# Attention and dense experts in one block: rows prepared tile by tile in attention's loop, first dense steps among its last slots

## The reference, cut to what matters

```
x = x + attention(layernorm(x), ctx)       # 16 heads, self and cross; LN; fp8 rounding of the
                                           # projections' inputs and of the head outputs
h = layernorm(x)                           # rows of x again: mean, variance, (x - m) * rstd
logits = h @ router_w                      # 8 experts, the best 2, softmax of the two
combined = sum over the row's 2 experts of score * (silu(h @ w1g[e]) * (h @ w1u[e])) @ w2[e]
shared = (silu(h @ w_gate) * (h @ w_up)) @ w_down      # "dense": every row, 1,024 wide
x = x + combined + shared
```

## Time and profile before

| | us |
|---|---|
| median of 3 runs (lowest, highest) | 1046.34 (1046.0, 1047.96) |
| the profiled execution, its own time | 1046.31 |
| its span in the trace | 1044.6 |
| PE busy | 960.6 (92%) |
| DVE busy | 796.8 (76%) |
| ACT busy | 737.8 (71%) |
| POOL busy | 434.2 (42%) |
| mean granted clock of TensorE | 0.972 |

### The profile page before, as it was taken

One profiled execution on the slowest core, in us unless ns is written; L12 is line 12 of the kernel. 1 busy time (PEld: TensorE's weight loads), 2 busy tenths in 40 slices (PEclk: granted clock), 3 DMA queues, 4 the chain that ended last, 5 costly groups with the idle time before them and its releaser, 6 DMA issues. The chain is left out here.

```text
span 1044.6 us, 23638 instructions
## 1 busy us (share of the span) xinstructions
PE 960.6 (92%) x7238; PEld 679.7 (65%) x7239; DVE 796.8 (76%) x1691; ACT 737.8 (71%) x1345; POOL 434.2 (42%) x642
## 2 busy tenths in 40 slices
PE   5487999999999999999999999859999799999994
PEld 3364777777777777777777777626565556666663
DVE  7677999999999999999999999766887634444441
ACT  6776888888888888888888878357455444454552
POOL 5223454445444544454445444270256013233222
PEclk9798999999999999999999999969999999999997
DMA  9924001010010010100100101041266364222222
GB/s 253 251 78 81 22 22 40 20 40 20 20 40 20 20 40 20 34 26 20 42 21 22 42 21 42 1 145 58 83 211 198 129 178 88 25 25 26 28 27 26
DMA packets 32821, 65.46 MB, mean 63 GB/s; under 512 B 3712, under 2 KB 20736, under 8 KB 32512
## 3 DMA queue, kind: packets, MB, share of 16 engines
q1 hardware_dynamic: 23312, 50.20, 15.4%
q0 software_dynamic: 9456, 14.59, 8.1%
HBM read 53.42 MB, written 16.59 MB: 67 GB/s over the span
## 5 line engine op out<-in xcount | busy, mean ns | idle before, releaser
L595 POOL TENSOR_TENSOR root<-vareps,neghalf 128x4 f32<-128x4 f32 (+1 forms) x128 | 173.7, 1357 | 10.0
L588 POOL TENSOR_TENSOR var<-ssq,unit 128x4 f32<-128x4 f32 (+1 forms) x128 | 52.6, 411 | 280.6 <-DVE ssq L455 280.6
L326 PE MATMUL b_pj<-w_hi,xq 128*128 128x512 f16 x384 | 148.7, 387 | 2.1 <-DVE xq L578 1.5
L399 ACT ACTIVATE sq<-b_pj 128x512 f32<-128x512 f32 x192 | 114.0, 594 | 50.6 <-PE b_pj L326 49.5
L326 PE MATMUL b_pj<-w_lo,xq 128*128 128x512 f16 x384 | 147.8, 385 | 0.0
L455 DVE TENSOR_REDUCE ssq<-sq 128x4 f32<-128x512 f32 x192 | 130.1, 678 | 11.2 <-ACT sq L399 11.1
L466 DVE TENSOR_TENSOR nrm<-raw,rstd 128x512 f32<-128x512 f32 x192 | 128.3, 668 | 5.1 <-POOL rstd L599 4.4
L1539 POOL DMA_INDIRECT out<-xg x39 | 60.5, 1552 | 169.2 <-ACT xg L1641 153.9
L352 PEld LDWEIGHTS b_sc<-kT,qT 128*128 128x128 f32 x1024 | 123.1, 192 | 7.2 <-ACT qT L425 0.3
L342 PE MATMUL b_tr<-ident,nrm 128*128 128x128 f32 x768 | 117.2, 276 | 9.7 <-DVE nrm L466 9.3
L352 PE MATMUL b_sc<-kT,qT 128*128 128x64 f32 x1024 | 121.5, 272 | 0.0
(11 more groups left out here) (291 smaller groups left out, 2288.0 us busy)
## 6 DMA issues: line engine op xcount, KB each, us to landing
nst<-in_ffw SPq DMA_DIRECT2D x30, 512.0 KB, 3.3
wload<-in_ffw SPq DMA_DIRECT2D x30, 512.0 KB
xbuf<-zero SPq DMA_DIRECT2D x39, 129.0 KB, 2.8
xg<-xbuf SPq DMA_DIRECT2D x9, 516.0 KB
x_sb<-in_x SPq DMA_DIRECT2D x4, 512.0 KB, 13.7
wproj<-in_ctxT SPq DMA_DIRECT2D x1, 2048.0 KB, 9.9
xq<-in_w_all SPq DMA_DIRECT2D x4, 512.0 KB, 21.3
wproj<-in_wprojT POOLq DMA_DIRECT2D x4, 512.0 KB, 8.9
```

What stands on the lines that cost most here:

```text
L326: last = pe.matmul(o, x, w[:, k, at:at + BANK], start=(k == 0 and n_ == 0), stop=(k == KT - 1 and n_ == len(terms) - 1))
L399: act.activation(sq[:, (r * NN + c) % 2, :], b_pj[c % 2][:, :], ACT.Square).then_inc(s["sq_done"], 1)
L595: pool.tensor_tensor(root[:, r % 2, c, :], vareps[:, r % 2, c, :], neghalf[:, 0:1].unsqueeze(2).to_broadcast(shape), ALU.pow).then_inc(s[" ...
```

## The change

- One block for attention and dense experts. The work on a tile's rows moves into attention's loop with offset `ROWS = -5`, one part per slot: in slots N%4 = 1 DVE's moments and then four POOL instructions (`pool_rows`); in N%4 = 2 the high half on ACT, the low half on DVE into `xr`; in N%4 = 3 four PE transposes into the bank of the probabilities and one ACT eviction into `xhl`. The router's four matmuls stand ahead of an output projection. `xr` goes to a DRAM buffer tile by tile; one 2,048 KB load brings all rows back as `xn`, behind weight piece 6 of SP's loads.
- The loop body is two tiles (8 slots), looped from slot 8 to 47, and the ring of quantised rows holds 2 tiles.
- The context is split in five parts: tile 0, then tiles 1 to 3, and 4, 4 and 4, one part in each of slots 0 to 3. Each quarter of `wproj`'s weights is loaded behind its part.
- Dense `up(0)` to `up(6)` go into slots 61 to 67, half behind "project 0", half behind "project 1"; `down(0)` into slot 65, 1 and 2 into 66, 3 and 4 into 67. They use attention's banks. Pieces 0 to 5 are split in slots 59 to 65, `silu` stands from slot 62 on, `product(n)` at the end of DVE's slot 62+n.
- In the dense steps left, the router's choice stands at step 7 (before 4), the end of the routing at 17 (before 14), weight pieces at steps 6, 7, 9, 10, 12 and up. A scatter waits for four dense steps more. `xg0` lies in the low half of `xhl` and waits for all dense ups and all scatters.

```diff
-        RING = 13
+        RING = 2
+        LOOPED = (2, 12)
...
+            def pe_rows(pe, t, part):
+                if part != 2:
+                    return
+                pe.wait_ge(s["xn_done"], t + 1)
+                after(pe, "xh_done", t)
+                after(pe, "ptev_done", min(4 * t + 8, 4 * NT) if isinstance(t, int) else 4 * t + 8)
+                for a in range(2):
+                    for k in range(KT):
+                        last = pe.transpose(b_t[:, a, k, :], xr[:, a * H + k * P:a * H + (k + 1) * P], ident16[:, :])
+                last.then_inc(s["t3_done"], 1)
...
-                    (0, "raw 2"): context_high,
+                    (0, "raw 2"): lambda: context_high(1), (1, "raw 2"): lambda: context_high(2),
+                    (2, "raw 2"): lambda: context_high(3), (3, "raw 2"): lambda: context_high(4),
...
+            def pool_rows(pool, t, part):
+                if part:
...
+                after(pool, "xn_done", t)
+                pool.wait_ge(s["mv3_done"], t + 1)
+                pool.tensor_tensor(ve3[:, :], mv3[:, 1:2], epsc[:, 0:1], ALU.add).then_inc(s["ve3"], 1)
+                pool.wait_ge(s["ve3"], t + 1)
+                pool.tensor_tensor(rs3[:, :], ve3[:, :], neghalf[:, 0:1], ALU.pow).then_inc(s["rs3"], 1)
+                pool.tensor_tensor(n3, row(x_sb, t), mv3[:, 0:1].to_broadcast([P, H]), ALU.subtract).then_inc(s["n3_sub"], 1)
+                pool.wait_ge(s["n3_sub"], t + 1)
+                pool.wait_ge(s["rs3"], t + 1)
+                pool.tensor_tensor(n3, n3, rs3[:, 0:1].to_broadcast([P, H]), ALU.mult).then_inc(s["n3_pool"], 1)
...
-            PIECE_SLOTS = (4, 6, 7) + tuple(range(11, NS))
+            PIECE_SLOTS = (6, 7, 9, 10) + tuple(range(12, NS))
...
                     sp.dma_start(stage[n % 3][:, :], ffw[n, :, :]).then_inc(s[f"wst_in{n % 3}"], 16)
+                    if n == 4:
+                        store_rows(sp, NT - 2)
+                    if n == 6:
+                        store_rows(sp, NT - 1)
+                        sp.wait_ge(s["row_out"], 16 * NT)
+                        sp.wait_ge(s["proj_done"], 16 * NT)
+                        sp.dma_start(xn[:, :, 0:2 * H].bitcast(U32), rowbuf).then_inc(s["rows_in"], 16)
                 sp.wait_ge(s["scattered"], 16 * 2 * NT)
-                sp.dma_start(xg0[:, :, :].bitcast(U32), x_rows[:, 0:TURN, :]).then_inc(s["xg_in"], 16)
+                sp.wait_ge(s["gu_done"], NS)
+                sp.dma_start(xg0.bitcast(U32), x_rows[:, 0:TURN, :])\
+                    .then_inc(s["xg_in"], 16)
...
-                        pool.wait_ge(s["gu_done"], (NT * slot + t) // 2 + 12)
+                        pool.wait_ge(s["gu_done"], (NT * slot + t) // 2 + 16)
...
+                def first_gate(n):
+                    def run():
+                        if n == 0:
+                            pe.wait_ge(s["xh_done"], 4)
+                            pe.wait_ge(s["raw_done"], 16 * NT)
+                        if n == 1:
+                            pe.wait_ge(s["tev_done"], NN * 4 * NT)
+                        pe.wait_ge(s["wl_done"], 2 if n < 4 else 4)
+                        after(pe, "a_done", n - 1)
+                        up_part(0, 0, n)
+                    return run
...
+                for n in range(JOIN + 1):
+                    tail[FIRST - 1 + n, "project 0"] = first_gate(n)
+                    tail[FIRST - 1 + n, "project 1"] = first_up(n)
+                tail[FIRST + 3, "project 3"] = downs(0)
+                tail[FIRST + 4, "first transposes"] = expert_sums
+                tail[FIRST + 4, "project 3"] = downs(1, 2)
+                tail[FIRST + 5, "project 3"] = downs(3, 4)
+                attention_tensor(pe, tail)
...
+                tail = {(FIRST - 3, "tokens"): shared(0), (FIRST - 2, "raw 1"): shared(1), (FIRST - 1, "raw 3"): units_known}
+                for n in range(JOIN):
+                    tail[FIRST + n, "first eviction"] = lambda n=n: gate(act, 0, n)
+                    tail[FIRST + n, "rows"] = lambda n=n: high(act, 0, n)
...
+                tail = {(FIRST - 2, "token norm"): shared(0), (FIRST - 2, "squares 2"): shared(1),
+                        (FIRST + 2, "tokens"): expert_scales}
+                for n in range(JOIN):
+                    if n:
+                        tail[FIRST + n, "token norm"] = lambda n=n: low(dve, 0, n - 1)
+                    tail[FIRST + n, "rows"] = lambda n=n: product(dve, 0, n)
+                for n in range(2, 6):
...
+                    (7, "weights"): choose, (8, "weights"): indices, (9, "weights"): marks,
+                    (10, "weights"): scores_and_counts, (11, "weights"): tile_scans,
+                    (12, "weights"): expert_scans, (13, "weights"): rows, (14, "weights"): tiles,
+                    (15, "weights"): codes, (16, "weights"): expert_units, (17, "weights"): expert_units_end,
                 })
```

More of the change, by code:

```diff
@@ L102, in rstd3 @@
[L102 to L108, removed]
+        st3 = sb("st3", [P, 6], F32)
+        mv3 = sb("mv3", [P, 2], F32)
+        ve3 = sb("ve3", [P, 1], F32)
+        rs3 = sb("rs3", [P, 1], F32)
@@ L271, in slots, with store_rows, attention_sync @@
                             between[N]()
-                        slot(N // 4, N % 4)
-                slots(-3, 4)
-                with eng.Fori(1, RING - 2) as i:
-                    for r in range(4):
-                        slot(i, r)
-                slots(4 * (RING - 2), 4 * NT + 3)
-            @block.sync
-            def _(sp):
+                        slot(N // 4, N % 4, N // 4 % 2)
+                first, end = LOOPED
+                slots(-3, 4 * first)
+                if 4 * first in between:
+                    between[4 * first]()
+                with eng.Fori(first, end, 2) as i:
+                    for r in range(8):
+                        slot(i + r // 4, r % 4, r // 4)
+                slots(4 * end, 4 * NT + 4)
+            def store_rows(sp, t):
+                sp.wait_ge(s["xn_done"], t + 1)
+                sp.dma_start(rowbuf[:, t, :], xr[:, :].bitcast(U32)).then_inc(s["row_out"], 16)
+            def attention_sync(sp):
                 sp.dma_start(col[:, :], cols).then_inc(s["cols_in"], 16)
@@ L1144, in ranks, with up_part @@
                     pe.matmul(b_rank, before, both.rearrange("p a b -> p (a b)"), start=True, stop=True)
-                    pe.matmul(b_tot, ones, both.rearrange("p a b -> p (a b)"), start=True, stop=True)\
+                    pe.matmul(b_tot, ones[:, :], both.rearrange("p a b -> p (a b)"), start=True, stop=True)\
                         .then_inc(s["rank_done"], 1)
+                def up_part(c, g, f):
+                    n = NF * g + f
+                    w, b = ((sw[0], b_g), (sw[1], b_u))[c]
+                    for k in range(KT):
+                        for m, (part, xx) in enumerate(((0, xh), (0, xl), (1, xh))):
+                            last = pe.matmul(b[f % 2][:, :], w[part][:, k * SF + f * P:k * SF + (f + 1) * P],
+                                             xx[:, k, g * BANK:(g + 1) * BANK],
+                                             start=(k == 0 and m == 0), stop=(k == KT - 1 and m == 2))
+                    if c:
+                        last.then_inc(s["gu_done"], 1)
                 def up(pe, g, f):
@@ L1174, in down, with downs @@
                     last.then_inc(s["ys_done"], 1)
-                def both_of(a, b):
+                def downs(*steps):
                     def run():
-                        if a is not None:
-                            route(a)
-                        if b is not None:
-                            turn(b)
-                    return run
-                pe.wait_ge(s["ones_set"], 1)
-                pe.wait_ge(s["wjob_done"], 1)
-                pe.matmul(b_wt, ones, wjob[:, :], start=True, stop=True).then_inc(s["wtot_done"], 1)
@@ L1750, in pieces, with halves @@
         return w.reshape(-1, PIECE // w.shape[1], P, w.shape[1]).transpose(0, 2, 1, 3).reshape(-1, P, PIECE)
+    def halves(w):
+        return w.reshape(KT, P, 2, SF // 2).transpose(2, 1, 0, 3).reshape(2, P, PIECE)
+    dense = [half for pair in zip(halves(w_gate), halves(w_up)) for half in pair]
     experts = [part for e in range(E) for part in (pieces(w1[e]), pieces(w2[e]))]
     arrays["router_w"] = np.ascontiguousarray(inputs["L0_ffn_router_w"])
-    arrays["ffw"] = np.ascontiguousarray(np.concatenate([pieces(w_gate), pieces(w_up), pieces(w_down)] + experts))
+    arrays["ffw"] = np.ascontiguousarray(np.concatenate([np.stack(dense), pieces(w_down)] + experts))
     nc = bacc.Bacc("TRN2", target_bir_lowering=False, num_devices=1)
```

561 lines of the change are left out of this document (270 added, 291 removed).

## The result

The changed kernel takes 1050.93 us (median of 8 runs, 1048.47 to 1052.29), the kernel before 1045.8 in the same sessions: ratio 1.0042 (1.0031 to 1.0053). It is slower by 5.1 us; 1031 was forecast. The profiled execution took 1050.13, with a span of 1048.2.

The account below looks back on a forecast made before the run. PE was taken to bound attention's loop, with stalls at the start and at the seam to dense. Start -6.7, loop +4.5, tail -13.6 and experts' first rows +0.3 gave -15.5 against 1046.31: 1031 us, range 1022 to 1042.

Parts of the forecast that it names:

- The loop: Attention's loop: PE gets four transposes (0.22) and four router matmuls (0.11) per tile, fourteen tiles in full slots: +4.5 us.
- POOL's rows: Row work on POOL in attention's loop: taken as hidden, 0; the rival that it throttles the loop had chance 0.14.
- The start: First slots: the context split in parts ends PE's wait for DVE's queue earlier: -6.7 us, bounds -4 to -10.2.
- The tail: From slot 61 through the dense steps: ups and downs fill attention's thinning slots, 159.8 against 173.4: -13.6 us, bounds -30.5 to -4.
- the chain: Slots 63 to 66: PE waits for DVE's products, the first queued last in slot 62: 11.4 us of waits.
- Table loads: ACT's switches of function tables in the tail: 1.28 us for a load, no extra drain counted in the sum.
- `xg0`: The experts' first rows, now waiting for all dense ups and scatters: +0.3 us, bounds 0 and 3.
- the reload of rows: The 2,048 KB load between weight pieces, ten steps ahead of the first scatter: 0, or 3 us if it delays piece 7.
- The slack of 4.6 for POOL's group: POOL's per-tile row group in the loop: hidden up to about 4.6 us by POOL's waits and PE's queue; loop stretches beyond 5.7.

Follow-up runs that it names:

- e12: Changed kernel with 32 idle wait instructions more on ScalarE ahead of its loop, body as long as before: 1036.97 us, ratio 0.9906 to the kernel before.
- e1: Changed kernel with ScalarE's loop body cut to one tile, the other engines keeping two: 1035.41 us, ratio 0.9903 to the kernel before.
- e7: Changed kernel with ScalarE's one-tile body, the product early, and all router matmuls moved from attention's loop to dense step 6: 1024.97 us.
- e4: Changed kernel with the dense product moved from the end of VectorE's slots 62 to 67 to ahead of the sum of the exponentials: 1038.82 us.
- e9: Changed kernel with ScalarE's one-tile body and four more 128x256 TENSOR_TENSORs on GpSimd per tile, written to an unread buffer: 1038.77 us.
- e3: Kernel before, with ScalarE's loop body alone made two tiles long: 1046.14 us, ratio 1.0002 to the kernel before.
- e5: Kernel before, with ScalarE's loop body two tiles long and 16 idle activations more in it: 1048.66 us, ratio 1.0023 to the kernel before.
- e10: Kernel before, with all engines' loop bodies two tiles long and no row work: 1047.05 us, ratio 1.0006 to the kernel before.
- e11: Changed kernel with GpSimd's loop body cut to one tile, the other engines keeping two: 1049.30 us, ratio 1.0024 to the kernel before.
- e17: Changed kernel with 40 idle waits (20 instructions) on ScalarE ahead of its loop: 1036.78 us, ratio 0.9911 to the kernel before.
- e14: Changed kernel with 130 idle wait instructions on ScalarE in slots 2 to 7, ahead of its loop: 1036.65 us, ratio 0.9908 to the kernel before.
- e16: Changed kernel with 512 idle waits (256 instructions) on ScalarE in slots 2 to 7, ahead of its loop: 1057.49 us, ratio 1.0109 to the kernel before.
- e2: Changed kernel with ScalarE's loop written out, without any jump back: 1035.37 us, ratio 0.9901 to the kernel before.
- e13: Kernel before, with ScalarE's body two tiles long, idle activations in it and idle waits ahead, placed at instructions 312 to 585: 1052.22 us.

## Why the prediction was wrong

- **The step that failed** is the loop's: "The loop ... +4.5". The list of the change named the loop body of two tiles, and I asked of it only which matmuls it adds. ACT's jump back was given no price at all: ACT's 68.5 us of idle time in 500 were read as room for the row work, while a wait of 3.3 in one piece passes through to PE. The jumps took 12.3 us in the trace; the versions without them are 14.0 (e12) to 15.5 (e1) faster in the medians, with the 1.7 of half clock in the traces' difference. None of my rivals had it: the one on the other side, POOL's rows, named another engine. What the Trainium skill says of jumps, in the section cited above, I had not weighed; that the wait depends on where the body lies, no row of before could have told.
- **The size of the loop's matmuls** was off as well: 7.8 for 4.5. The router's four take 0.25 per tile, not 0.11 (e7), and the whole work 0.53 a tile, not 0.33; a wait of 0.67 in slot 59 behind the first weight piece on DVE adds about a microsecond.
- **The start**: the mechanism was right, the size 4.9 for 6.7. A slot of DVE with a part took 10.16 (maxima at 93.67 and 103.83), not 9.57, and I had left out that it waits 0.4 to 1.3 for ACT's `y` there.
- **The tail**: right in place and cause, and 12.8 for 13.3 in size, with PE's waits 9.0 for 11.4. How close the size came is in part luck: in e1's trace, without the half clock in dense step 9, the same stretch gives 14.5. That I called the chain a given, not a fault, is another matter: e4 moves one line and gains 12.1.
- **Table loads, `xg0`, the reload of rows, POOL's rows**: nothing visible, as taken. The slack of 4.6 for POOL's group was not worked out from its rows, which add up to 3.01 + 1.03 = 4.04, with DVE's 0.40 to 4.44; e9's group of 4.8 agrees with it all the same.
- Without the jumps the change is near what it was read to be: e1 is at 1035.4, e12 at 1037.0, inside the range of 1022 to 1042 and 4 to 6 above its 1031.

```profile
93.67 0.68 DVE L534 TENSOR_REDUCE mx<-b_sc 128x8 f32<-128x512 f32 x1
...
103.83 0.68 DVE L534 TENSOR_REDUCE mx<-b_sc 128x8 f32<-128x512 f32 x1
```

## What to carry to other kernels

When a hardware loop's body grows, count each engine's instructions in it, waits and register moves too, and look in the trace for instruction loads and for waits for `issue` at the first instruction of the body. A long body alone need not cost anything (e3, e5, e10): the same body waits at one place of the program and not at another, so an edit ahead of the loop can bring the waits or take them away. An engine that needs no unrolling can loop over a shorter body on its own. And where work is interleaved into a chain, the result that the bottleneck engine waits for goes to the front of its slot, not behind the work that nobody waits for.

## What the runs showed of the hardware

- A loop body of 275 instructions on ScalarE waited 3.2 to 3.7 us at each jump back at one place of its program (the changed kernel, e4, e11), and not at all 20, 32 or 130 instructions further on (e17, e12, e14); at 256 the wait was back (e16). VectorE's body of 311 and TensorE's of 646 instructions never waited at theirs in these runs, each at one place only; VectorE's of 309 in e10 waited 0.3 at each of its three jumps.
- Where such a body waits, instruction loads recur on every pass (ten in 160 us); the kernel before has none in that stretch, nor has e17, and e2, with the loop written out, has three. Code written out was loaded without a wait, but for single ones of 1.6 to 1.7 us (one before, three in e17) and those among the idle waits of e13, e14 and e16.
- Behind the same wait of 1.96 of TensorE the granted clock of the next 10 us was 0.83 in five traces and 1.00 in eight; the first costs 1.7 us.
- A TENSOR_TENSOR of 128x256 on GpSimd takes 0.61 to 1.12 us, against 1.22 to 1.82 for the TENSOR_SCALARs of before; four in a row take 2.77.
